# A fused two-layer perceiver: 16-head attention by query tiles, the 4-head attention's first pair entered early, bias rows on Pool, side steps in new places

## Chip, cores and metric

The kernel runs on one core of a Trainium2 chip. The metric is the device time of one execution in microseconds. Before the change the median of 3 runs is 592.93 (592.2 to 593.36).

## What is computed

The input `x` (2 batches of 256 rows, 256 wide, float32) goes through two layers; each step adds its result to `x`:

```python
x = x + xattn0(layernorm(x), ctx)        # scores over 4096 context rows per batch, values = ctx
x = x + linear_attention(layernorm(x))   # 64 heads of 4, cumulative sums
x = x + feed_forward(layernorm(x))       # 3 cycles of a gelu net that couples the two halves
x = x + xattn1(layernorm(x), ctx)
x = x + attn16(layernorm(x))             # 16 heads of rank 64: softmax(xQ (xK)^T / 16) x VO_h, summed
x = x + ffn(layernorm(x))
```

The last step is:

```python
def _mha(x, w, b, ow, ob):               # x is (L, N, D); attention runs over L
    L, N, _ = x.shape
    q, k, v = jnp.split(x @ w.T + b, 3, axis=-1)       # then 4 heads of 64
    attn = softmax(q k^T / sqrt(64))
    return (attn @ v) @ ow.T + ob
y1 = _ln(x + _mha(x, ...), ln1_g, ln1_b)
y2 = _ln(y1 + _moe(y1, ...), ln2_g, ln2_b)   # top-1 router, 8 experts of 64 places each
```

Here L is 2, the batches. So the 4-head attention of a row needs only the same row of the other batch: rows 0 to 127 of both batches are one pair of tiles (tiles 0 and 2, pair 0), rows 128 to 255 the other (tiles 1 and 3, pair 1). The 16-head attention needs all rows of its batch as keys, and each row only as a query.

## The kernel before, in words

All five engines have their own program; they meet at semaphores. The stages, with their times in the profiled execution:

- 0 to 30 us: start. Then **attention 0** to about 167 us: `attend(0, ...)` goes through 64 steps (`ORDER`), each a score or a value step of a query tile and a context chunk. Into it are put side steps: generators (`project`, `linear_attention`, `feed_forward`) of which `side_steps` advances one `yield` at the half steps that `SIDE_AT` lists for PE, ACT and DVE, each by itself. `PREP_AT` says at which steps ACT and DVE cut the next chunk of the context into two float16 halves; SP loads it, and turns it by DMA behind the cut.
- To about 218 us: **between**. Batch 0's side steps run out (the last feed-forward cycle, `project("y", 0)`), and batch 1's linear attention runs, in the order that the strings `BETWEEN` give for each engine ("y" is a step of batch 0's chain, "a" one of batch 1's).
- To about 347 us: **attention 1**, with batch 1's feed-forward, its projection and the entry of the 16-head attention as side steps. Then its projections, to about 369 us.
- To about 495 us: the **16-head loop** (`low_rank_attention`, PE from L641), 32 heads: 16 of batch 0, then 16 of batch 1, in 36 steps of a software pipeline. In step i PE does `scores5(i)` (two heads at a time, when i is even), `turn5(i-2)`, `mix5(i-3)` and `out5(i-4)`; DVE does the maximum, norm and low halves (`max5`, `norm5`, `lo5`, `oT_lo`), ACT the exponentials and high halves, Pool the low halves of the output weights. The outputs of all heads of a batch add up in one PSUM bank (6 or 7).
- Batch 0's rows leave this loop early. From step 20 on each engine advances its generator `enter_last` once at the end of each step (PE L759, DVE L1587): read of the bank and residual (`leave(0)`), layer norm, turn, and the projections of tiles 0 and 1 to q, k and v (PE L771 to L783, DVE L1562), through bank 6, in two pieces of 512 and 256 columns each.
- **The tail**, 495 to 535 us: `leave(1)` (L1551), layer norm "m" of batch 1 (L1270; Pool computes the reciprocal root, L1189), turn of tiles 2 and 3, their projections (PE L792 and L794). Then for each pair j: projection's bias add (L1623), products of queries and keys (pair 0 on DVE, pair 1 on Pool, L310), `scores6(j)` (L1628 to L1632), exponential on ACT, `values6(j)` (L1637 to L1647), turn (`turn_pair`, L756), output projection (L806), residual, output bias (L1664, L1665), statistics, norm (`norm_apply`, L1602 and L1606, with the root from Pool, L1245). DVE adds the bias of the second norm to X at L1658. After both pairs: turn, router's logits (L820), which DVE reads at L1677.
- To 592 us: **experts**: routing, and four pairs of experts, each with a matmul from 256 to 1024 (L864), a turn (L875), and one from 1024 to 256 (L889); combining (L898), second norm, store.

`keep_busy(n, bank)` (L410) issues n matmuls whose result nobody reads. What sets the order around the change are the programs of the engines themselves: everything behind a waiting instruction waits too. On SP's queue the weights of the last layer are loaded in program order behind the semaphores of L380 to L396. The memory of the expert weights 0 to 5 (`w2`, in `ctx_tr`) is that of the 16-head loop's tensors.

## Time and profile before

| | us |
|---|---|
| median of 3 runs (lowest to highest) | 592.93 (592.2 to 593.36) |
| the profiled execution | 593.91 |
| its span (first to last instruction) | 591.7 |
| PE busy | 522.6 (88%) |
| DVE busy | 366.1 (62%) |
| ACT busy | 282.7 (48%) |
| POOL busy | 70.1 (12%) |

PE is TensorE, DVE VectorE, ACT ScalarE, POOL GpSimd, SPq the queue in which SyncE issues DMAs. The time lies 2.2 us above the span: start and end of the execution. In the rows below "L732" is a line of the kernel; `out<-in` names what is written and read; a releaser behind `<-` in brackets is what ended the idle time before the instruction.

### The profile page before, as it was taken

To read this page: it belongs to the slowest core of one execution; us is meant where nothing else is said; L and a number is where in the kernel's file an instruction comes from. 1 tells how busy PE (TensorE), PEld (TensorE's weight loads), DVE (VectorE), ACT (ScalarE), POOL (GpSimd) and SP (SyncE) were. 2 spreads that over 40 slices of the span, in tenths; PEclk is the share of its full clock that TensorE was granted. 3 is DMA by queue.
4 is the path that set the end of the run, shared out by engine and by line. 5 is a ranking of instruction groups with operands and counts; after the bars stand their busy time and mean duration, and the time that the engine had idled before them with its cause. 6 is when DMAs were issued, how large, how long until landed. Compare 5 with 4: busy or idle time off the path is not lost.

```text
span 591.7 us, 9246 instructions
## 1 busy us (share of the span) xinstructions
PE 522.6 (88%) x3492; PEld 357.2 (60%) x3492; DVE 366.1 (62%) x855; ACT 282.7 (48%) x610; POOL 70.1 (12%) x59
## 2 busy tenths in 40 slices
PE   8599998999984779999989989699999998868993
PEld 6356664456642445657545777488888786654552
DVE  4665557864558555556465555688878773874335
ACT  3567852438812016674367736888554451012100
POOL 0114231200012100000002212333000000110001
PEclk9989999999996789999999999699999999989998
DMA  5658670000000010000320041221760136640001
GB/s 191 214 183 213 143 150 28 1 1 1 1 0 0 1 27 2 0 2 1 134 80 1 1 143 37 71 74 37 240 246 2 39 105 214 214 143 0 1 1 35
DMA packets 45196, 44.04 MB, mean 74 GB/s; under 512 B 18656, under 2 KB 41184, under 8 KB 45024
## 3 DMA queue, kind: packets, MB, share of 16 engines
q1 hardware_dynamic: 45152, 43.45, 23.8%
q8 instruction: 28, 0.46, 0.3%
q14 instruction: 16, 0.13, 0.1%
HBM read 38.73 MB, written 0.52 MB: 66 GB/s over the span
## 4 chain that ended last, share of the span: by engine, by line
PE 68%; DVE 16%; issue 8%; ACT 5%; DMA 2%; POOL 0%; SPq 0%; DVEq 0%; ACTq 0%; POOLq 0%
PE ps L590 9%; PE ps L720 7%; PE ps L619 7%; PE ps L732 7%; PE ps L604 4%; PE ps L621 4%; PE ps L679 4%; PE ps L706 3%; PE ps L864 2%; PE ps L889 2%; PE ps L694 2%; PE ps L483 2%; PE ps L437 2%; DVE work L1361 1%; DMA work<-in_ctx 1%
## 5 line engine op out<-in xcount | busy, mean ns | idle before, releaser
L590 PE MATMUL ps<-ctx_tr,qtl 128*128 128x512 f16 x384 | 91.7, 382 | 2.6 <-ACT arena L1039 2.1
L1427 DVE TENSOR_REDUCE mx<-arena 128x1 f32<-128x512 f32 x64 | 43.4, 683 | 34.2 <-ACT arena L1039 34.0
L590 PEld LDWEIGHTS ps<-ctx_tr,qtl 128*128 128x128 f16 x384 | 37.2, 99 | 41.5 <-issue 5.1
L1039 ACT ACTIVATE arena<-ps 128x512 f32<-128x512 f32 x64 | 38.0, 595 | 48.3 <-PE ps L590 48.2
L619 PE MATMUL ps<-ctx_nat,pth 128*128 128x512 f16 x172 | 58.2, 379 | 0.0
L1024 ACT ACTIVATE arena<-arena,small 128x512 f32<-128x512 f32 x64 | 45.8, 715 | 6.0 <-DVE small L1436 6.0
L732 PE MATMUL ps<-arena,ctx_tr 128*128 128x256 f16 x384 | 47.2, 273 | 0.1
L621 PE MATMUL ps<-ctx_nat,ptl 128*128 128x256 f16 x172 | 46.9, 273 | 0.0
L1189 POOL TENSOR_TENSOR rstd<-mv,col 128x2 f32<-128x2 f32 x12 | 9.2, 769 | 289.6 <-DVE mv L1280 289.6
L1441 DVE TENSOR_TENSOR ptl<-ps,pth 128x512 f16<-128x512 f32 x43 | 29.6, 689 | 22.3 <-ACT pth L1032 22.0
L604 PE MATMUL ps<-const,arena 128*128 128x128 f32 x256 | 39.0, 275 | 5.0 <-ACT arena L1024 2.8
L732 PEld LDWEIGHTS ps<-arena,ctx_tr 128*128 128x128 f16 x384 | 37.5, 98 | 4.7 <-DVE ctx_tr L1572 0.4
L604 PEld LDWEIGHTS ps<-const,arena 128*128 128x128 f32 x256 | 29.9, 140 | 16.7 <-ACT arena L1024 6.7
L1111 ACT ACTIVATE pth<-ps 128x512 f16<-128x512 f32 x32 | 19.0, 594 | 35.6 <-PE ps L706 35.6
L1104 ACT ACTIVATE ctx_tr<-ps,small 128x256 f32<-128x256 f32 x64 | 29.6, 470 | 5.9 <-DVE work L1531 5.9
L1032 ACT ACTIVATE pth<-ps 128x512 f16<-128x512 f32 x43 | 25.3, 589 | 13.3 <-PE ps L604 13.2
L1572 DVE TENSOR_TENSOR ctx_tr<-ps,ctx_tr 128x512 f16<-128x512 f32 x32 | 22.0, 689 | 13.0 <-ACT ctx_tr L1117 13.0
L1531 DVE TENSOR_SCALAR_CACHE_REDUCE work<-ps 128x256 f16<-128x256 f32 x64 | 24.4, 419 | 9.2 <-PE ps L694 9.1
L619 PE MATMUL ps<-ctx_nat,arena 128*128 128x512 f16 x84 | 28.6, 379 | 0.0
L619 PEld LDWEIGHTS ps<-ctx_nat,pth 128*128 128x128 f16 x172 | 16.8, 98 | 16.4 <-issue 0.4
L1441 DVE TENSOR_TENSOR arena<-ps,arena 128x512 f16<-128x512 f32 x21 | 14.5, 689 | 16.5 <-ACT arena L1032 16.3
L1544 DVE TENSOR_SCALAR ctx_tr<-ctx_tr,small 128x256 f32<-128x256 f32 x64 | 23.7, 412 | 1.1
(289 smaller groups left out, 1056.5 us busy)
## 6 DMA issues: line engine op xcount, KB each, us to landing
work<-in_ctx SPq DMA_DIRECT2D x16, 512.0 KB, 3.7
ctx_nat<-in_w_e SPq DMA_DIRECT2D x8, 1024.0 KB, 7.4
ctx_tr<-in_w_e SPq DMA_DIRECT2D x6, 1024.0 KB, 11.9
work<-in_w_vo SPq DMA_DIRECT2D x8, 512.0 KB, 3.8
ctx_nat<-in_w_l SPq DMA_DIRECT2D x4, 512.0 KB, 5.2
arena<-in_w_e SPq DMA_DIRECT2D x2, 1024.0 KB, 7.2
wts<-in_rows SPq DMA_DIRECT2D x1, 1024.0 KB, 7.2
arena<-in_w_a SPq DMA_DIRECT2D x1, 768.0 KB, 5.0
```

The costliest lines, as they stand in the source:

```text
L590: mm = pe.matmul(ps[:, n % 2, :], qtl[:, qh, d, u * P:(u + 1) * P], CT[:, t0:t0 + KT, kh, d, :], start=(i == 0 and d == 0), stop=(i == 2 a ...
L604: mm = pe.transpose(ps[:, 4 + j % 2, i * P:(i + 1) * P], S[:, (j) % SRING, i * P:(i + 1) * P], ident)
L619: pe.matmul(ps[:, acc, :], PH[j % PRING][:, i * P:(i + 1) * P], CN[:, t].rearrange("p h d -> p (h d)"), start=(c == 0 and i == 0), stop=Fa ...
L621: mm = pe.matmul(ps[:, acc, 0:D], PL[j % PRING][:, i * P:(i + 1) * P], CN[:, t, 0, :], start=False, stop=(c == NCH - 1 and i == KT - 1), s ...
L720: mm = pe.matmul(ps[:, 4 + i % 2, d * SEQ:(d + 1) * SEQ], xl5[b][:, xh, u, d * P:(d + 1) * P], pt[:, i % 2, pu], start=(n == 0), stop=(n = ...
L732: mm = pe.matmul(ps[:, 6 + b, t * D:(t + 1) * D], oT5[:, i % 2, oh, c, t * P:(t + 1) * P], vo[:, h, vh, c, :], start=(h == 0 and t == 0 an ...
L1024: act.activation(S[:, j % SRING, :], S[:, j % SRING, :], ACT.Exp, bias=ebias[:, u:u + 1], scale=SCALES[L], accum_out=ls[:, u, c:c + 1]).th ...
L1032: act.activation(PH[j % PRING], ps[:, 4 + j % 2, :], ACT.Copy).then_inc(s("pt_hi"), 1)
L1039: act.activation(S[:, n % SRING, :], ps[:, n % 2, :], ACT.Copy).then_inc(s("score_copied"), 1)
L1104: act.activation(P5[:, i % 2, t, :], ps[:, i % 2, t * SEQ:(t + 1) * SEQ], ACT.Exp, bias=nb5[:, i % 2, t:t + 1], scale=1.0 / 16, accum_out= ...
L1427: dve.tensor_reduce(mx[:, u, c:c + 1], S[:, n % SRING, :], AX.X, ALU.max).then_inc(s("score_max"), 1)
L1441: dve.tensor_tensor(PL[j % PRING], ps[:, 4 + j % 2, :], PH[j % PRING], ALU.subtract).then_inc(s("pt_lo"), 1)
```

## The change

It has five parts.

- **Query tiles.** For batch 1 the loop's step i no longer holds both query tiles of one head but one query tile of two heads: `in_step(i, p)`. The first 8 steps of batch 1 do tile 2 for all 16 heads, the last 8 do tile 3. The number of matmuls, turns and reads per step stays. PE waits for DVE's read of tile 2 (`x5`) before it writes tile 3's first output.
- **Pair 0 inside the loop.** `enter_last` goes on behind tiles 0 and 1: DVE reads tile 2 (`leave(1, slice(0, 1), H5 + 8)`), norms it, PE turns and projects it, Pool multiplies queries and keys of pair 0, DVE does `scores6(0)` and `values6(0)`, ACT the exponential, PE turn and output projection. The steps of each engine are placed by `LAST_AT` (half steps 0 to 71 of the loop) instead of one per step. The tail then holds tile 3's norm and projection, pair 0's residual and norm, and pair 1.
- **Pool** adds the output bias to `x0` and the second norm's bias to `X` (`biases`), six adds; DVE's adds at L1665 and L1658 go. Pool's product is now pair 0's, DVE computes pair 1's.
- **Side steps**: `SIDE_AT`, `BETWEEN`, `PREP_AT` have new numbers, and `Y0_AT` is 2: Pool's root for "y", 0 stands behind the second product of the linear attention of batch 1, not ahead of it.
- **Matmuls that keep PE busy**: 24, 56 and 36 become 18, 6, 30, 0 and 30. Tensors `P5`, `oT5`, `xl5[1]` and `prods[0]` lie elsewhere, and SP loads `w2[4]` and `w2[5]` behind the last head's output.

The diff, cut to what the text speaks of:

```diff
-Y0_AT = 1
+FILL = (18, 6, 30, 0, 30)
+LAST_AT = (
+    (49, 50, 51, 54, 55, 58, 59, 62, 70, 71,),
+    (65, 70,),
+    (43, 47, 48, 48, 50, 52, 54, 55, 55, 56, 57, 60, 62, 64, 67, 69,),
+)
+Y0_AT = 2
...
-PREP_AT = [0, 1, 2, 3, 4, 5, 6, 7, 9, 13, 15, 22, 24, 28, 30]
+PREP_AT = [0, 1, 2, 3, 4, 5, 6, 7, 9, 12, 13, 24, 27, 30, 31]
...
-            (1, 2, 4, 11, 16,),
-            (1, 2, 4, 11, 16,),
-            (1, 2, 5, 11, 16,),
+            (1, 3, 4, 11, 16,),
+            (0, 2, 4, 13, 16,),
+            (2, 2, 5, 12, 16,),
...
-    "yayaaayayaayyayyaaayyaaaa",
-    "aaayyayayaayayyaaayyaa",
-    "aaayyyaayaayayayayayayaaa",
+    "aayyayaaaayyyyayaaayyaaay",
+    "aaayaaaaaaaaayayayaaaayy",
+    "ayyaayaaaayyayyayayaayaaaa",
...
+        def in_step(i, p):
+
+            k = i - H5
+            return (i // 2, p) if k < 0 else (k % 8 // 2 * 2 + p, k // 8)
...
-            sp.wait_ge(s("l_vo"), H5 + H5 // 2)
+            sp.wait_ge(s("l_vo"), 2 * H5 - 4)
             load_w2(6)
             load_w2(7)
             sp.wait_ge(s("l_pv"), 2 * H5)
-            for e in range(6):
+            for e in range(4):
+                load_w2(e)
+            sp.wait_ge(s("l_vo"), 2 * H5)
+            for e in range(4, 6):
                 load_w2(e)
             sp.wait_ge(s("m_o"), 2)
...
+                    for p in range(2):
+                        j, t = in_step(i, p)
...
+                    pe.wait_ge(s("vo_lo"), min(i + 1, H5))
+                    if i == H5 + 8:
+                        pe.wait_ge(s("x5"), 2)
...
+                    for _ in range(LAST_AT[PE].count(2 * i)):
+                        next(early, None)
...
+            def leave_pair(j, b_turn, b_out):
+                pe.wait_ge(s("m_o"), j + 1)
+                turn_pair(o6, 0, b_turn, "m_oT_ps", j)
+                yield
+                pe.wait_ge(s("m_oT"), j + 1)
+                for b in range(B):
+                    t = 2 * b + j
+                    for c in range(DC):
+                        mm = pe.matmul(ps[:, b_out, b * D:(b + 1) * D], oT6[:, c, t * P:(t + 1) * P],
+                                       w6o[:, c, :], start=(c == 0), stop=(c == DC - 1))
+                mm.then_inc(s("m_out"), 1)
+                yield
+
             def enter_last():
...
+                for n in range(6):
                     t, cols = n // 2, ((0, 512), (512, 768))[n % 2]
-                    if n:
+                    if n == 4:
+                        turn_latents(1, (2,), 6)
+                        yield
+                    if n in (0, 4):
+                        pe.wait_ge(s("m_xT"), n // 4 + 1)
+                    else:
...
+                yield from leave_pair(0, 6, 6)
...
+                keep_busy(FILL[0], 2)
+                turn_latents(2, (3,), 3)
+                keep_busy(FILL[1], 2)
+                pe.wait_ge(s("m_xT"), 3)
+                for c in range(DC):
...
+                mm.then_inc(s("m_qkv_ps"), 1)
+                first_tiles()
+                for _ in leave_pair(1, 7, 3):
+                    pass
...
+            def first_tiles():
+                keep_busy(FILL[2], 2)
+                tiles_to_logits(0)
+                keep_busy(FILL[3], 2)
 
...
+            def biases(k, tiles):
+
+                w = [P, tiles.stop - tiles.start, D]
+                pool.wait_ge(s("w6_in"), 16 * 14)
+                pool.wait_ge(s("xn_turned"), NORM["m", k] + 1)
+                pool.tensor_tensor(x0[:, tiles, :], x0[:, tiles, :], b6o.unsqueeze(1).broadcast_to(w), ALU.add).then_inc(s("x_bo"), 1)
+                pool.tensor_tensor(X[:, tiles, :], X[:, tiles, :], ln2b.unsqueeze(1).broadcast_to(w), ALU.add).then_inc(s("x_beta"), 1)
+
+            layernorm("m", 0)
+            biases(0, slice(0, 2))
+            layernorm("m", 1)
+            biases(1, slice(2, 3))
+            pool.wait_ge(s("m_qkv0"), 6)
+            queries_times_keys(pool, 0).then_inc(s("m_prod"), 1)
+            layernorm("m", 2)
             for k, pair in enumerate((slice(0, NT, 2), slice(1, NT, 2), slice(0, 2), slice(2, 4))):
                 pool.wait_ge(s("m_var"), k + 1)
                 pool.tensor_tensor(rstd4[:, pair], mv4[:, pair, 1], nh, ALU.pow).then_inc(s("m_rstd"), 1)
+                if k == 0:
+                    biases(2, slice(3, 4))
 
 
...
+                def enter_last():
+                    dve.tensor_copy(ones16, ones[:, :])
+                    dve.tensor_copy(tris16, tris)
+                    dve.tensor_copy(id16, ident).then_inc(s("id16"), 1)
+                    leave(0, slice(0, 2), H5)
+                    yield
+                    yield from latents(0, (0, 1), 6)
+                    yield
+                    dve.wait_ge(s("w6_in"), 16 * 14)
+                    yield from project_early(range(4))
+                    leave(1, slice(0, 1), H5 + 8)
+                    yield from latents(1, (2,), 6)
+                    yield
+                    yield from project_early((4, 5))
+                    dve.wait_ge(s("m_prod"), 1)
+                    scores6(0)
+                    yield
+                    values6(0)
+                    yield
 
                 early = enter_last()
...
+                leave(1, slice(1, 2), 2 * H5)
+                entry = latents(2, (3,), 3)
+                next(entry)
+                for _ in early:
+                    pass
+                next(entry)
+                residual(0, 6)
+                for _ in entry:
+                    pass
...
+            def residual(j, n):
+                dve.wait_ge(s("m_out"), j + 1)
+                dve.wait_ge(s("x_bo"), B + 2 + j)
+                xs = x0[:, j:NT:2, :]
+                link(dve.tensor_tensor(xs, xs, bank(n, a=2), ALU.add))
+                norm_stats(x0, j, (j, 2 + j))
...
+                first_norm = norm_apply(x0, 0, (0, 2), ln1g, x0, lambda t: ln1b)
+                next(first_norm)
+                dve.wait_ge(s("m_qkv_ps"), 1)
+                link(dve.tensor_tensor(qkv[:, 3, :], ps[:, 0:2, :].rearrange("p b n -> p (b n)")[:, 0:768], b6i, ALU.add))
+                link(queries_times_keys(dve, 1))
                 scores6(1)
+                publish(next(first_norm), "m_y1")
                 values6(1)
+                residual(1, 3)
+                second_norm = norm_apply(x0, 1, (1, 3), ln1g, x0, lambda t: ln1b)
+                next(second_norm)
+                publish(next(second_norm), "m_y1")
```

## Rows read from the trace of the kernel before

**Rows 1.** Windows by stage: stretch, busy us (and instructions) of each engine, PEclk, DMA.

```profile
30.00:160.00 130.00, 123.24 (x707) 75.56 (x705) 80.50 (x152) 80.33 (x156) 23.68 (x13) 0.99 0.34 82
160.00:218.00 58.00, 38.41 (x133) 22.98 (x132) 34.21 (x67) 9.51 (x16) 6.63 (x5) 0.82 0.03 7
218.00:347.00 129.00, 123.61 (x706) 76.29 (x704) 72.57 (x150) 76.47 (x161) 11.28 (x11) 1.00 0.10 32
381.00:496.00 115.00, 114.90 (x1071) 97.36 (x1068) 89.85 (x275) 70.65 (x194) 12.25 (x11) 1.00 0.31 107
```

**Rows 2.** Chain of waits in the tail: start us, us, what.

```profile
493.78 1.50 PE ps L732 x12
495.30 0.70 DVE X L1551
...
497.75 0.70 POOL rstd L1189
...
505.36 0.97 DVE ctx_nat L1623
...
507.61 1.23 DVE work L1628
...
521.79 3.43 PE ps L806 x8
525.24 0.70 DVE ctx_tr L1664
...
527.84 0.88 DVE ctx_tr L1602 x2
```

**Rows 3.** Timeline of DVE in the tail: start us, us, instruction.

```profile
510.71 2.05 DVE L1639 TENSOR_TENSOR work<-work 128x16 f32<-128x16 f32 x1
...
517.72 0.16 DVE L1637 TENSOR_TENSOR work<-work 128x8 f32<-128x8 f32 x1
...
519.69 0.69 DVE L1647 TENSOR_TENSOR ctx_tr<-ctx_tr,arena 128x512 f32<-128x512 f32 x1
...
534.64 0.18 DVE L1677 COPY work<-ps 128x32 f32<-128x32 f32 x1
```

**Rows 4.** Chain of waits, projection of tile 0 in the loop.

```profile
455.64 1.72 PE ps L780 x4
```

**Rows 5.** Timeline of PE: pair 0 in the tail.

```profile
514.87 0.66 PE L756 MATMUL ps<-const,ctx_tr 128*128 128x128 f32 x4 [0.92 <-DVE ctx_tr L1647]
516.21 1.99 PE L806 MATMUL ps<-work,ctx_tr 128*128 128x256 f32 x8 [0.69 <-ACT ctx_tr L1138]
```

**Rows 6.** Windows ahead of and at the second output projection; PEclk follows POOL.

```profile
518.20:521.80 3.60, 0.67 (x6) 0.44 (x5) 3.46 (x6) 0.60 (x1) 0.00 (x0) 0.93 0.24 26
521.80:525.30 3.50, 3.50 (x11) 2.80 (x12) 1.26 (x7) 0.00 (x0) 0.69 (x1) 0.58 0.86 335
```

**Rows 7.** Timeline of POOL: the product of pair 1.

```profile
510.38 2.35 POOL L310 TENSOR_TENSOR arena<-ctx_nat 128x1024 f32<-128x1024 f32 x1 [11.94 <-DVE ctx_nat L1623]
```

**Rows 8.** Timeline of PE between the attentions, idle before in brackets.

```profile
187.65 1.11 PE L549 MATMUL ps<-const,arena 128*128 128x128 f32 x4 [8.04 <-DVE arena L1404]
...
195.68 0.66 PE L420 MATMUL ps<-const,wts 128*128 128x128 f32 x4 [2.65 <-DVE wts L1286]
198.09 3.78 PE L437 MATMUL ps<-arena,wts 128*128 128x256 f32 x8 [1.75 <-DVE arena L1293]
```

**Rows 9.** Timeline of DVE: the second tile's keys are ready.

```profile
188.67 0.42 DVE L1348 TENSOR_TENSOR work<-work,s 128x256 f32<-128x256 f32 x1
```

**Rows 10.** Timeline of POOL between the attentions.

```profile
191.83 2.01 POOL L1206 TENSOR_TENSOR work<-work 128x1024 f32<-128x1024 f32 x1
```

**Rows 11.** Timeline of PE in attention 0: wait for a score copy.

```profile
103.05 2.32 PE L590 MATMUL ps<-ctx_tr,qtl 128*128 128x512 f16 x10 [2.09 <-ACT arena L1039]
```

**Rows 12.** Timeline of SP's queue: issues of w2 0 to 5.

```profile
492.39 11.81 SPq L360 DMA_DIRECT2D ctx_tr<-in_w_e  x6
```

**Rows 13.** Chain of waits: first matmuls on w2.

```profile
552.58 3.45 PE ps L889 x31
```

More of the change, by code:

```diff
@@ new lines, in last_attention, with tiles_to_logits @@
+                for c in range(DC):
+                    mm = pe.matmul(ps[:, 1, 0:D], x0T[:, c, 3 * P:4 * P], w6i[:, c, 512:768], start=(c == 0), stop=(c == DC - 1))
+                mm.then_inc(s("m_qkv_ps"), 1)
+                first_tiles()
+                for _ in leave_pair(1, 7, 3):
+                    pass
+            def tiles_to_logits(j):
+                pe.wait_ge(s("m_y1"), j + 1)
+                turn_pair(x0, j, 4, "m_yT_ps", j)
+                pe.wait_ge(s("m_yT"), j + 1)
+                for t in (j, 2 + j):
@@ L791, in last_attention @@
                     for c in range(DC):
[L792 to L794 removed]
+                        mm = pe.matmul(ps[:, 6, t * E6:(t + 1) * E6], x0T[:, c, t * P:(t + 1) * P], wgt[:, c, :],
                                        start=(c == 0), stop=(c == DC - 1))
[L796 removed]
@@ L810, in experts @@
[L810 to L822 removed]
+                return mm
@@ L1132, in y_hi @@
                     act.activation(yy[:, g, 0], ys, ACT.Copy).then_inc(s("m_y_hi"), 1)
-                for j in range(2):
-                    act.wait_ge(s("m_sub"), j + 1)
-                    act.activation(sc[:, j], sc[:, j], ACT.Exp, scale=HD6 ** -0.5).then_inc(s("m_exp"), 1)
-                    act.wait_ge(s("m_oT_ps"), j + 1)
-                    act.activation(by_batch(oT6, j), ps[:, 6 + j, :].rearrange("p (c b n) -> p c b n", c=DC, b=B), ACT.Copy)\
-                        .then_inc(s("m_oT"), 1)
+                second = leave_pair(1, 7)
+                next(second)
                 for j in range(2):
@@ L1143, in last_part @@
                         .then_inc(s("m_yT"), 1)
-                for j in range(2):
-                    act.activation(y1[:, 0, j:NT:2, :], x0[:, j:NT:2, :], ACT.Copy).then_inc(s("m_y1_hi"), 1)
+                    if j == 0:
+                        next(second)
+                    else:
+                        for k in range(2):
+                            act.activation(y1[:, 0, k:NT:2, :], x0[:, k:NT:2, :], ACT.Copy).then_inc(s("m_y1_hi"), 1)
                 act.wait_ge(s("m_sub8"), 1)
@@ L1266, in _, with layernorm @@
             C = lambda name, n=P: col[0:n, COL[name]:COL[name] + 1]
-            def layernorm(what, b, to=None):
+            def layernorm(what, b, to=None, tiles=None):
                 k = NORM[what, b]
@@ L1273, in layernorm @@
                     dve.wait_ge(s("x_in%d" % b), 16)
-                for t in range(2):
-                    last = dve.bn_stats(bst[:, t, :], X[:, 2 * b + t, :])
+                tiles = (2 * b, 2 * b + 1) if tiles is None else tiles
+                for t, x in enumerate(tiles):
+                    last = dve.bn_stats(bst[:, t, :], X[:, x, :])
                 link(last)
-                for t in range(2):
+                for t in range(len(tiles)):
                     last = dve.bn_aggr(mv[:, t, :], bst[:, t, :])
@@ L1284, in layernorm @@
                     dve.wait_ge(s("xn_turned"), k)
-                for t in range(2):
-                    last = dve.tensor_scalar(to[:, t, :], X[:, 2 * b + t, :], mv[:, t, 0:1], rstd[:, t:t + 1],
+                for t, x in enumerate(tiles):
+                    last = dve.tensor_scalar(to[:, t, :], X[:, x, :], mv[:, t, 0:1], rstd[:, t:t + 1],
                                              ALU.subtract, ALU.mult)
@@ L1579, in low_rank_attention @@
                         norm5(i - 1)
+                    for _ in range(LAST_AT[DVE].count(2 * i)):
+                        next(early, None)
                     if 2 <= i <= 2 * H5 + 1:
```

229 lines of the change are left out of this document (85 added, 144 removed), and 12 rows, old and new, of the table SIDE_AT.

## The prediction, made before the changed kernel ran

> **What bounds the kernel now.** I read the time by stage first. In the three long stages TensorE is the bound: it is busy 123.2 of 130 us, 123.6 of 129 and 114.9 of 115 [rows 1]. The last of these is the loop of the 16-head attention; there DVE has 25 us free (89.9 of 115) and PE nothing. So side work put into that loop costs what it takes on PE, and what it takes on DVE is free while that slack lasts. Two stretches differ: the one between the two big attentions (PE 38.4 of 58 us) and the tail behind the loop, where the chain of waits runs from one engine to the next. The chain [rows 2] starts at T = 493.78 us with the last head's twelve matmuls and reaches the router's logits on DVE at 534.64 [rows 3]: 40.9 us for two pairs of query tiles, the second behind the first.
>
> **Part 1: the loop gets longer.** Tile 2 is projected in it (two matmul groups) and turned, and pair 0 is finished in it. The same projections of tiles 0 and 1 cost 1.72 us for 512 columns [rows 4], so about 0.86 for 256; turning one tile is half of 0.66 [rows 5]. Sum 2.9 us, all on PE, all on the path. On DVE the added steps are a few reads and norms of one tile, two bias adds, the scores (1.23 + 0.4 us) and the values of pair 0 (from 517.72 to the end of the 0.69 at 519.69, 2.66 us) [rows 2, 3]: together about 8 us (estimate), against 25 free. I followed the three step lists from step 25 on. PE meets no late operand until the end. There `values6(0)` stands ahead of the last head's `oT_lo`, and the turn of pair 0 ahead of the last head's matmuls: 1.0 us more before T. Bounds: 0.5 (the turn alone) and 2.7 (all of `values6`). The new wait of step 24's output on `x5` holds one PE queue, but DVE's read is asked for one step (about 3 us) earlier (114.9 us of PE for 36 steps): nothing. If that cover goes, it is a read of 0.5 us. Loop: +3.9 us. That scores and outputs go by query tiles leaves 12 matmuls for each two heads and 12 per head as they were: nothing.
>
> **Part 2: the tail from T.** Step by step, from rows:
> - last matmuls to DVE's first read: 1.5 (493.78 to 495.30).
> - read, statistics and epsilon up to Pool's power: 2.45 now for two tiles with three casts in between. One tile, without casts: 1.4, between 1.2 (half) and 2.45. Then Pool 0.7 and one tile's normalization 0.4. T + 4.0.
> - residual of pair 0 with its statistics: 525.24 to 527.84 is 2.6, less one add of 0.7 that moves to Pool: 1.9. Its operand, pair 0's projection, takes 2.0 on PE behind the last head and is ready. T + 5.9.
> - copy of tile 3 (0.4, half width) and its projection at the full clock, 2.6 + 0.2: T + 9.1. The first half of the norm of pair 0 and Pool's power and two adds lie beside it.
> - projection's add and the product of queries and keys: 505.36 to 507.61, 2.25; scores 1.65: T + 13.0.
> - second half of pair 0's norm 0.9, values of pair 1 2.66: T + 16.6.
> - turn and ACT's copy: 514.87 to 516.21, 1.34 [rows 5]: T + 17.9.
> - its eight matmuls: 1.99 at one clock [rows 5], 3.43 at the other [rows 2].
> - residual 1.9, norm in two halves 0.9 each, then 3.2 from the norm to the logits: 527.84 plus four halves is 531.4, and the logits are read at 534.64 [rows 2, 3].
> With 3.43 this is T + 28.3, so 12.6 less than 40.9; with 1.99 it is 14.0 less. I take 3.43: in the kernel before, PE was busy 0.67 of the 3.6 us ahead of such matmuls and the granted clock then fell to 0.58, the level of 1.2 GHz for most of it [rows 6]; in the changed order PE has about 2 us of work in the 5.6 us between its filler matmuls and these. **Loop and tail together: -8.7** (-10.1 with the full clock).
>
> **Part 3: Pool's adds.** Two adds of 128x512 leave DVE's chain for the output bias (0.7 each, in the sums above) and two for the second norm's bias, which lay where DVE waited for ACT. On Pool they are six: two of 512 and four of 256 columns. The nearest row is Pool's product of 1024 columns, 2.35 us [rows 7], so 1.2 and 0.6 each, 4.8 us in all, behind nothing that is due. Queued behind them are the power of tile 2's norm (six steps later) and the product of pair 0. What the row also shows: DVE's small multiply beside that product took 2.05 us instead of 0.2, and ended when Pool did [rows 3, 7]. In the loop Pool gets 3.6 us of adds and 2.35 of product, so DVE could be held 6 us; it has the slack, so I take nothing. The Trainium skill has a page that speaks against the change here: "SBUF — State Buffer", on who interferes with whom, says that a DVE instruction with two SBUF inputs or in a two-port mode is fully blocked while GpSimd reads SBUF. The row agrees with it; by that rule taken at its worst the sum is the rival B below.
>
> **Part 4: side steps placed anew.** In the stretch between the attentions PE waits 8.04 us for the last feed-forward cycle, then 2.65 for the next norm, then 1.75 [rows 8]. Now Pool multiplies the second tile's keys and values only after a power that waits for a later variance: DVE had its operand at 189.1, Pool began at 191.83 [rows 9, 10]. With Y0_AT = 2 the multiply goes first and the power starts about when it did. DVE normalizes ahead of the first running sum's reads, so PE turns that norm straight behind its sums at 193.0: the wait of 2.65 goes. The wait of 1.75 comes next and grows by 0.2, because the copy then stands behind DVE's reads. The 8.04 stays but for about 0.5 us, as the third feed-forward matmul is moved ahead of a projection. I take **-2.5**; bounds 0 and -3.2.
> Within the two big attentions PE idles 6.8 and 5.4 us in all [rows 1], of which a gain can be at most a part. Against it stands that a side step can block: at 103.05 PE had waited 2.09 us for a score copy, as ACT stood at a side step [rows 11]. No row prices the new places; I take nothing, and -4 to +4 for the range. The last two cuts of the context come two and three steps later in ACT's order, some 3 us; the scores that need them come seven steps on, so nothing.
> DMAs: experts' weights 4 and 5 now wait for the last head's output instead of its mixing, about 3 us later in SP's queue, and 6 and 7 for four heads more. The six loads were issued in 11.8 us from 492.39, and the first matmul on such weights ran at 552.58 [rows 12, 13]: even 10 us nearer they are covered. Nothing; if the cover went, the cost would be what the loads run past that matmul.
>
> **Sum.** -8.7 - 2.5 = -11.2 us on the profiled execution's 593.91 (span 591.7): 582.7. The median of the runs, 592.93, is 1.0 below it, so I forecast 581.7.
>
> **Rivals.**
> - A, the forecast: 577 to 585. Chance 0.62.
> - B, the port: Pool's reads hold DVE in the loop when a head is due, and the 6 us of part 3 all reach PE. 587.7. For: the 2.05 us row. Against: the loop's slack on DVE. Chance 0.11.
> - C, the new places inside the attentions cost what the stretch between gains, and some of the tail: 585 to 590, worked out as -11.2 + 2.5 + 2 = 586.2. Chance 0.12.
> - D, everything fits: full clock in the tail and 3 us out of the attentions' idle time, 577.3 and less. Chance 0.08.
> - E, slower: ACT stops at side steps ahead of score copies, 2.1 us on PE each time as at 103.05 [rows 11]. Six such stops more than before, one in every fifth or so of the 30-odd moved steps, cost 12.6 us: 594.3. From the sixth on it decides. For: three lists are moved and not all alike. Against: the kernel before has one such stop. Chance 0.04.
> - F, pair 0 isn't really inside the loop. Its turn and projection are PE's steps 70 and 71, at the last head. If `values6(0)` runs late, its 4.7 us of turn, copy and matmuls stand behind the loop: 586.4. Chance 0.03, and it counts with C. Of C's chance 0.03 lies beyond 591.7, where its price is double: 0.02 there is the same, 0.01 slower.
> The range takes A, B and most of C and D: 577.0 to 588.5. A measurement of this kernel can tell about 0.2%, 1.2 us, from no change: faster 0.93, same 0.02, slower 0.05.
>
> **What would show it.** Right: the loop without PE idle and 3 to 5 us longer; from the last head's matmuls to the logits 27 to 29 us; one projection of tile 3 in the tail; PE's turn of the second norm straight behind the running sum. Wrong: idle PE at the turns or mixes in the loop released by DVE (B); a span from 30 to 160 or 218 to 347 longer by over 2 us (C, E); in the tail a wait for pair 0's projection (F) or 1.2 GHz in tile 3's projection, 2.6 us more.

## The result, and the profile after

The changed kernel takes 578.27 us (577.6 to 582.76) against 592.57 before on the same chip: a ratio of 0.9756, 95% interval 0.9726 to 0.9785. The profiled execution took 577.76 us (span 575.9), half a microsecond under the median; 582.7 was the sum and 581.7 the forecast. Against the profiled execution of before, the span is 15.8 us shorter, 4.6 more than the 11.2 of the sum.

I cut both traces at the same instructions: the first turn of attention 0, a feed-forward matmul behind it, the last feed-forward cycle, the first score and the last turn's end of attention 1, the loop's start, T, and the logits on DVE. Windows by stage of the kernel before, columns as in [rows 1]:

```profile
49.57:136.89 87.32, 83.26 (x449) 48.43 (x449) 57.01 (x109) 48.29 (x99) 19.43 (x11) 1.00 0.35 79
136.89:187.65 50.76, 38.91 (x206) 24.75 (x205) 27.69 (x56) 27.55 (x54) 3.96 (x3) 0.96 0.00 0
187.65:217.65 30.00, 21.89 (x63) 13.92 (x63) 16.81 (x33) 1.19 (x2) 2.67 (x2) 0.73 0.05 14
...
373.88:493.78 119.90, 119.25 (x1085) 99.58 (x1085) 93.39 (x290) 76.15 (x208) 14.83 (x14) 0.97 0.30 101
493.78:534.64 40.86, 32.43 (x204) 24.60 (x205) 27.84 (x60) 3.86 (x8) 4.57 (x4) 0.92 0.62 206
```

And of the changed kernel:

```profile
47.47:133.57 86.10, 83.25 (x448) 48.37 (x448) 56.73 (x109) 48.46 (x101) 19.47 (x11) 1.00 0.38 80
133.57:183.06 49.49, 39.17 (x205) 24.89 (x205) 27.70 (x56) 24.70 (x50) 3.96 (x3) 0.94 0.00 0
183.06:209.96 26.90, 20.77 (x63) 13.38 (x64) 17.03 (x33) 1.08 (x2) 2.71 (x2) 0.75 0.05 15
...
366.12:489.81 123.69, 121.93 (x1098) 101.06 (x1098) 100.11 (x310) 76.49 (x210) 21.77 (x20) 0.98 0.30 99
489.81:518.72 28.91, 23.84 (x156) 18.79 (x157) 16.38 (x39) 3.61 (x7) 3.86 (x5) 0.93 0.86 285
```

The second number of a row is the length of its stretch. The loop grew by 3.79 us, and PE's busy time in it by 2.68. The granted clock of the two loops isn't the same (0.97 and 0.98); the section on the prediction sets this against loops of the same clock. The tail fell by 11.95. The three stretches ahead of 218 us fell by 1.22, 1.27 and 3.10. Ahead of the first turn 2.10 went; attention 1 and the experts' part moved by 0.1.

The chain of waits in the tail of the changed kernel can be laid beside part 2 of the prediction term by term (start us, us, what):

```profile
489.07 0.70 DVE ctx_tr L1652
...
489.81 1.50 PE ps L751 x12
...
491.34 0.44 DVE X L1611
...
492.73 0.71 POOL rstd L1235
...
493.79 0.69 DVE ctx_tr L1705
...
496.12 1.98 PE ps L831 x4
...
499.08 0.97 DVE ctx_nat L1735
...
506.63 0.67 PE ps L780 x4
...
507.98 3.60 PE ps L799 x8
...
511.66 0.70 DVE ctx_tr L1705
```

From T = 489.81 the first read comes at +1.5, pair 0's residual at +4.0, the add of the projection at +9.3, the turn of pair 1 at +16.8, the end of its projection at +21.8 and the logits at +28.9. The projection of pair 1 ran at 1.2 GHz, 3.60 us, as the sum had it.

### The profile page after: what moved, and what is told of

Read it like the earlier page. It is cut to its first block, busy times and chain, and to the rows that moved or that the text cites. A ratio compares the mean times of both kernels' runs of the same rounds, so it can differ in the third digit from the quotient of the medians.

```text
span 575.9 us, 9191 instructions
## 1 busy us (share of the span) xinstructions
PE 516.6 (90%) x3460; PEld 352.3 (61%) x3460; DVE 360.7 (63%) x855; ACT 279.7 (49%) x608; POOL 75.4 (13%) x66
## 4 chain that ended last, share of the span: by engine, by line
PE 67%; DVE 16%; issue 8%; ACT 5%; DMA 2%; POOL 1%; SPq 0%; DVEq 0%; ACTq 0%; POOLq 0%
PE ps L604 9%; PE ps L633 8%; PE ps L751 7%; PE ps L735 7%; PE ps L635 4%; PE ps L618 4%; PE ps L693 4%; PE ps L721 3%; PE ps L899 3%; PE ps L924 2%; PE ps L709 2%; DMA work<-in_ctx 2%; PE ps L819 1%; DVE mx L1487 1%; DVE work L1421 1%
## 5 line engine op out<-in xcount | busy, mean ns | idle before, releaser
L1501 DVE TENSOR_TENSOR ptl<-ps,pth 128x512 f16<-128x512 f32 x43 | 29.5, 688 | 22.7 <-ACT pth L1067 22.5
L1139 ACT ACTIVATE ctx_tr<-ps,small 128x256 f32<-128x256 f32 x64 | 29.6, 470 | 5.2 <-DVE work L1591 5.2
L633 PEld LDWEIGHTS ps<-ctx_nat,pth 128*128 128x128 f16 x172 | 16.8, 98 | 16.7 <-issue 1.0
L1501 DVE TENSOR_TENSOR arena<-ps,arena 128x512 f16<-128x512 f32 x21 | 14.5, 690 | 18.0 <-ACT arena L1067 17.9
L1282 POOL TENSOR_TENSOR arena<-work,arena 128x512 f16<-128x512 f32 x16 | 18.5, 1155 | 46.9 <-ACT arena L1119 46.9
```

The source lines that it names most:

```text
L633: pe.matmul(ps[:, acc, :], PH[j % PRING][:, i * P:(i + 1) * P], CN[:, t].rearrange("p h d -> p (h d)"), start=(c == 0 and i == 0), stop=Fa ...
L1139: act.activation(P5[:, i % 2, t, :], ps[:, i % 2, t * SEQ:(t + 1) * SEQ], ACT.Exp, bias=nb5[:, i % 2, t:t + 1], scale=1.0 / 16, accum_out= ...
L1501: dve.tensor_tensor(PL[j % PRING], ps[:, 4 + j % 2, :], PH[j % PRING], ALU.subtract).then_inc(s("pt_lo"), 1)
```

## The experiments

Ratios are to the kernel before, run beside each group; its own median lies between 592.0 and 593.8 us from group to group, so terms are read in the stretches of the traces. The changed kernel's 0.9756 is the mark, and where the interval of a ratio overlaps its interval (0.9726 to 0.9785), the ratio alone doesn't tell the two apart.

**1. The four lists of places back in the changed kernel.**

SIDE_AT and BETWEEN too are those of the kernel before, and:

```diff
-Y0_AT = 2
+Y0_AT = 1
...
-PREP_AT = [0, 1, 2, 3, 4, 5, 6, 7, 9, 12, 13, 24, 27, 30, 31]
+PREP_AT = [0, 1, 2, 3, 4, 5, 6, 7, 9, 13, 15, 22, 24, 28, 30]
```

> The changed kernel with the four old lists of places (before the loop it is then the kernel before, in the loop and the tail the changed one). Theory: the profiles differ by 7.7 us ahead of the loop (first turn 2.1 earlier, attention 0 another 1.9, between the attentions 3.7), and the new places make all of it: this run is 7.7 us slower than the changed kernel, about 585.5, and its gain over the kernel before, 8 us, is the tail and the loop alone. Rival 1: the 2.1 us ahead of the first turn are the landing times of the inputs and no work of the places: 5.6 us slower, 583.5. Rival 2 (my prediction's terms): only the stretch between gains, 2.5: 580.5.

0.9864 (0.9827 to 0.9901): 8.1 us less than before, 6.4 more than the changed kernel. The loop and the tail together take what they take in the changed kernel (152.6 us, against 160.8 before: 8.2 us), so this part stands by itself. The first turn started at 48.74.

**2. The same lists in the kernel before.**

> The kernel before with the four new lists of places. Theory: the same 7.7 us, 585 against 592.7, and the loop and the tail as they were (119.9 and 40.9 us). Rival 1 (landing times): 587. Rival 2: 590. If this and the run with the old places give different gains, the parts are not independent, and the profile has to show where one leans on the other.

0.9908 (0.9875 to 0.9941), 5.5 us less; loop and tail 160.7 us, as before. The two halves add up: 8.1 + 5.5 = 13.6, against 14.5 for the change (2.44% of 592.57). From the first turn to the first score of attention 1 it takes 162.6 us, the changed kernel 162.5, experiment 1 166.3 and the kernel before 168.1. So the places are worth 4 to 5.6 us there. That leaves the 2.1 ahead of the first turn. Experiment 4 shows where 4 and 5.6 part.

**3. The start and the two halves of attention 0.** The changed kernel with PREP_AT and the first lists of before, and with the second lists of before:

```diff
-            (1, 3, 4, 11, 16,),
-            (0, 2, 4, 13, 16,),
-            (2, 2, 5, 12, 16,),
+            (1, 2, 4, 11, 16,),
+            (1, 2, 4, 11, 16,),
+            (1, 2, 5, 11, 16,),
...
-            (66, 66, 69, 71, 72, 72, 74, 75, 77, 80, 83, 83, 87, 88, 90, 96, 97, 99, 99, 103, 104, 104, 105, 107, 110,
+            (63, 66, 69, 71, 71, 71, 72, 74, 75, 80, 82, 86, 87, 88, 88, 95, 96, 96, 97, 102, 104, 105, 105, 107, 108,
...
```

> The changed kernel with PREP_AT and the lists of the first half of the first attention (SIDE_AT[0][0]) of before. In all profiles with the new lists the first turn starts at 46.6 to 49.4 us (eight kernels, mean 47.6), with the old ones at 48.7 and 49.6; the first attention behind it, up to a feed-forward matmul at 133 us, takes 86.1 with the new and 87.3 with the old. Theory: the start is the landing of the inputs and not the lists, and the 1.2 us are these lists (the waits for cuts): first turn anywhere from 46.6 to 49.6, then 87.3, and about 1.2 us slower in all. Rival: the 1.2 us are the second half's lists: 86.1 here.

> The changed kernel with the lists of the second half of the first attention (SIDE_AT[0][1]) of before. Theory: the 1.3 us between the feed-forward matmul at 133 and the last wait of 8 us (49.5 us with the new places, 50.8 with the old) are these lists, and nothing else moves: 1.3 us slower. Rival: those come from the lists of the stretch between: 49.5 here, and no slower.

0.9782 (0.9743 to 0.9822) and 0.9806 (0.9774 to 0.9837). The rival of the first holds: with the first lists of before, the stretch up to the feed-forward matmul is still 86.1 us; with the second lists it is 87.3, and up to the last feed-forward cycle 137.3 us from the first turn, against 135.6 changed and 138.1 before. So the second lists made 1.7 of those 2.5 us. Where they did shows in PE's waits of more than 0.25 us between the first turn and the last cycle's: they add up to 6.52 us with the second lists of before and to 4.52 in the changed kernel. Timelines of PE with the second lists of before, then of the changed kernel (idle before in brackets; four of its waits each):

```profile
104.51 3.40 PE L573 MATMUL ps<-ctx_tr,qtl 128*128 128x512 f16 x15 [2.08 <-ACT arena L1043]
...
143.01 0.65 PE L517 MATMUL ps<-wts 128*64 128x256 f32 x2 [0.36 <-ACT wts L993]
...
163.53 0.65 PE L517 MATMUL ps<-wts 128*64 128x256 f32 x2 [0.96 <-ACT wts L993]
...
164.73 0.70 PE L526 MATMUL ps<-wts 64*128 64x256 f32 x2 [0.56 <-ACT wts L999]
```

```profile
98.19 1.46 PE L604 MATMUL ps<-ctx_tr,qtl 128*128 128x512 f16 x6 [0.88 <-ACT arena L1074]
100.69 3.40 PE L604 MATMUL ps<-ctx_tr,qtl 128*128 128x512 f16 x15 [1.05 <-ACT arena L1074]
...
136.50 1.13 PE L541 MATMUL ps<-wts 128*128 128x256 f32 x4 [0.59 <-ACT wts L1017]
...
156.38 1.13 PE L541 MATMUL ps<-wts 128*128 128x256 f32 x4 [0.28 <-ACT wts L1017]
```

The first wait is that of [rows 11], which I had used against the change. The new places hardly shorten it: 2.08 us in one piece became 0.88 and 1.05. The gain lies later, in the feed-forward's waits for ACT: 0.36, 0.96 and 0.56 became 0.59 and 0.28. Another 0.75 us of the 2.5 is still gained with the second lists of before. There PE waits 0.21 us for DVE ahead of one of the feed-forward's matmul groups, where the kernel before waits 0.79. The lists of the stretch between are the likely cause; no run has them alone.

The start is little or no part of the change. With one and the same set of first lists, profiled executions started their first turn anywhere from 46.6 to 51.0 us (eleven of them, half at 47.5 or earlier: the changed kernel 47.47, the kernel of experiment 6 with the same lists 49.40); with the old ones it was 48.74, 49.57 and 50.60. Three against eleven can't rule out a part of the lists in it. But the timed medians gave 14.3 us, and the trace has 13.7 behind its first turn, which leaves about half a microsecond for the start. What differs is, in part at least, how long ACT waits for the DMA of a context tile. Timelines of ACT, changed kernel and experiment 6:

```profile
25.37 1.06 ACT L1047 ACTIVATE ctx_nat<-work 128x1024 f16<-128x1024 f32 x1 [2.61 <-DMA work<-in_ctx]
```

```profile
25.86 1.06 ACT L1051 ACTIVATE ctx_nat<-work 128x1024 f16<-128x1024 f32 x1 [3.73 <-DMA work<-in_ctx]
```

**4. Y0_AT alone back at 1.**

> The changed kernel with only Y0_AT back at 1, so that Pool's power comes ahead of its second multiplication. Theory (the prediction's): the wait of 2.65 us for the second norm's turn went through this, and comes back, about 2 to 2.5 us: 580.5. Rival: the lists of the stretch between (DVE's norm ahead of its reads of the running sum) made it, and Pool's order is nearly free: within 0.5 us of the changed kernel.

0.9817 (0.9788 to 0.9845). Timelines of PE, and of Pool and DVE, between the attentions, this run, to be read against [rows 8]:

```profile
182.67 1.12 PE L563 MATMUL ps<-const,arena 128*128 128x128 f32 x4 [8.09 <-DVE arena L1464]
183.57 4.04 PE L497 MATMUL ps<-work,const 128*128 128x512 f32 x6
189.38 0.66 PE L434 MATMUL ps<-const,wts 128*128 128x128 f32 x4 [1.77 <-DVE wts L1346]
```

```profile
186.85 2.00 POOL L1252 TENSOR_TENSOR work<-work 128x1024 f32<-128x1024 f32 x1
186.92 2.41 DVE L1346 TENSOR_SCALAR wts<-X,mv,rstd 128x256 f32<-128x256 f32 x2 [0.82 <-POOL rstd L1235]
```

The turn of the norm comes 6.7 us behind the turn of the feed-forward cycle's result, in the changed kernel 5.2. So Y0_AT is worth 1.5 us beside the new lists, but not in the way predicted. The two normalizations of that norm, which DVE does right behind Pool's power, take 2.41 us here, and 0.74 in the changed kernel: the first began 0.07 us behind Pool's product of 1024 columns and ended 0.14 behind it. With Y0_AT = 2 the product is over before the power, and nothing holds them. Experiment 7 brings this hold about on purpose.

The strings of BETWEEN do their part too. With the old ones DVE normalizes behind its reads of the running sums, and the turn stands 2.65 us behind the six matmuls of those sums, however long they take: 4.47 us in the profile of before (turn at 8.0 us), 3.26 in experiment 1 (turn at 6.8), at other granted clocks. With the new ones DVE normalizes ahead of those reads, and the turn came at 5.16 or 5.17 us in all eleven kernels that have the new strings of BETWEEN and Y0_AT at 2, while their sums took 3.3 to 4.5 us. So the two together are worth 2.9 us against the profile of before and 1.7 against experiment 1. That is most of what parts 5.6 from 4 us in experiment 2.

**5. More fillers at one place.**

```diff
-FILL = (18, 6, 30, 0, 30)
+FILL = (18, 6, 44, 0, 30)
```

> The changed kernel with 44 instead of 30 filler matmuls ahead of the turn of pair 0's norm in the tail. In the changed kernel PE is idle there until 505.6 us and the eight matmuls of pair 1's projection then take 3.59 us at 1.2 GHz, against 1.99 at 2.4. Theory: with PE busy up to the turn the clock stays up and the projection takes 2.0: 1.5 us faster, 576.8. Rival 1: the idle stretch behind the turn (1.7 us of work in 2.4) lowers the clock all the same: 0. Rival 2: the fillers run beyond the moment at which the norm is ready and delay it: 0.5 us slower.

0.9782 (0.9762 to 0.9803), no gain. PE is now busy up to the turn of pair 0's norm at 504.62, but for 0.16 us, and the granted clock still falls behind it: the turn of pair 1 takes 1.11 us instead of 0.66. The idle pieces of PE between the fillers and that turn are 0.16, 0.69 and 0.30 us. From T to the logits it takes 29.56 us, what experiment 4 took too, whose tail is that of the changed kernel and whose clock was as low (0.88 over the stretch, against 0.93 in the changed kernel's 28.91). Timeline of PE:

```profile
507.32 1.11 PE L780 MATMUL ps<-const,ctx_tr 128*128 128x128 f32 x4 [0.30 <-DVE ctx_tr L1699]
509.12 3.78 PE L799 MATMUL ps<-work,ctx_tr 128*128 128x256 f32 x8 [0.69 <-ACT ctx_tr L1172]
```

**6. Fillers in every gap.**

```diff
+FILL = (18, 6, 44, 2, 30)
                 turn_pair(x0, j, 4, "m_yT_ps", j)
+                if j == 0:
+                    keep_busy(5, 2)
...
                 turn_pair(o6, 0, b_turn, "m_oT_ps", j)
+                if j:
+                    keep_busy(5, 2)
```

> The changed kernel with filler matmuls in each gap of PE from the projection of tile 3 to pair 1's output projection: 44 ahead of the turn of pair 0's norm, 5 behind it, 2 behind the first logits, 5 behind the turn of pair 1. 44 alone did not keep the clock: the eight matmuls took 3.78 us at a granted clock of 0.50, after 0.82 in the 2 us before. Theory: what lowered it are the gaps of 0.7 to 1.7 us behind that turn; with these filled the projection takes 2.0 us: 1.6 us less from the last head to the logits than 28.9. Rival: the fall doesn't hang on these gaps, or the fillers themselves stand in the way of the turns (0.1 to 0.3 us each): 0 or slower by up to 0.5.

0.9714 (0.9688 to 0.9739). This interval still overlaps the changed kernel's. But experiment 8, which measured the same as the changed kernel, ran on the same chip: its times are 578.1 to 580.5 us, those of this one 575.3 to 577.8, so this one is faster. From T to the logits it takes 27.3 us instead of 28.9, the 1.6 expected, at a granted clock of 1.00. Timeline of PE, and the windows at the projection (columns as in [rows 1]):

```profile
506.95 1.06 PE L849 MATMUL ps<-wts,ctx_tr 128*128 128x8 f32 x8
507.87 0.38 PE L424 MATMUL ps<-ones 128*128 128x256 f16 x2
508.31 0.66 PE L780 MATMUL ps<-const,ctx_tr 128*128 128x128 f32 x4
508.81 0.71 PE L424 MATMUL ps<-ones 128*128 128x256 f16 x5
509.65 1.99 PE L801 MATMUL ps<-work,ctx_tr 128*128 128x256 f32 x8
```

```profile
508.00:510.00 2.00, 1.79 (x14) 1.20 (x12) 0.26 (x1) 0.60 (x1) 0.00 (x0) 1.00 0.77 236
510.00:512.00 2.00, 2.00 (x13) 1.68 (x12) 0.26 (x1) 0.00 (x0) 0.00 (x0) 1.00 1.00 368
```

**7. The port: twelve more products on Pool in the loop.**

```diff
+            busy = prods[0].rearrange("p (a b) -> p a b", a=8)
+            one = ident.unsqueeze(1).broadcast_to([P, 8, P])
+            for k in range(12):
+                pool.tensor_tensor(busy, one, one, ALU.mult).then_inc(s("busy"), 1)
+                pool.wait_ge(s("busy"), k + 1)
```

> The changed kernel with twelve more products of 1024 columns on Pool in the loop, right behind its last subtraction of a head (406.8 us), which read and write SBUF: 12 x 2.35 = 28 us of Pool, over before the power at 444.5. All else is as it was. Theory (the prediction's): DVE's instructions in the loop mostly read PSUM and are not held, and where one is held DVE's slack of 25 us takes it: 0, and no PE idle between 405 and 436. Rival (the port, B of the prediction): DVE is held while Pool reads; with the lag that six microseconds were to give priced at one for one, 28 us of Pool cost up to 28, and a few us at least, and PE's idle time in that stretch shows DVE as releaser.

0.9937 (0.9905 to 0.9969): the loop takes 133.6 us instead of 123.7. My theory fell, the rival's mechanism is real. Timeline of DVE (out and in are named; `small` holds the softmax divisors):

```profile
410.87 3.92 DVE L1610 TENSOR_SCALAR ctx_tr<-ctx_tr,small 128x256 f32<-128x256 f32 x2
414.72 0.68 DVE L1602 TENSOR_TENSOR ptl<-ps,pth 128x512 f16<-128x512 f32 x1
```

The two normalizations, which read and write SBUF and take 0.62 us for both in quiet parts of the loop, take 3.92, two whole Pool products of 1.97 each. The next instruction, which takes an operand from PSUM, is as long as ever (0.68). So one pair per head is held, by up to the length of two Pool instructions, and PE waits for it, 2.52, 1.76 and 2.52 us ahead of three turns of the loop that DVE's normalization releases: in 405 to 430 us PE is busy 18.1 of 25, where it is busy all 25 in the changed kernel. The price depends less on Pool's total than on what it runs when a normalization is due.

In the changed kernel itself the new Pool work misses those moments. Timeline of DVE and POOL, changed kernel:

```profile
478.33 2.35 POOL L321 TENSOR_TENSOR ctx_nat<-ctx_nat 128x1024 f32<-128x1024 f32 x1 [8.71 <-DVE ctx_nat L1625]
479.65 0.69 DVE L1652 TENSOR_TENSOR ctx_tr<-ps,ctx_tr 128x512 f16<-128x512 f32 x1 [0.80 <-ACT ctx_tr L1152]
...
480.45 0.64 DVE L1604 TENSOR_SCALAR ctx_tr<-ctx_tr,small 128x256 f32<-128x256 f32 x2
```

The longest of the normalizations beside its adds and its product took 0.71; beside Pool's subtractions for the heads, in the first third of the loop of both kernels, it is up to 1.31. The Trainium skill's page "SBUF — State Buffer", on who interferes with whom, says that where such instructions of DVE and GpSimd meet, the one that issues first has the shared ports for its whole length and the other is fully blocked; my prediction had quoted it without the order. The trace agrees: here the Pool product was the first, and the pair took 3.92 us.

**8. The bias rows on DVE.**

```diff
+                    dve.tensor_tensor(x0[:, ts, :], x0[:, ts, :], b6o.unsqueeze(1).broadcast_to(to), ALU.add).then_inc(s("x_bo"), 1)
+                    dve.tensor_tensor(X[:, ts, :], X[:, ts, :], ln2b.unsqueeze(1).broadcast_to(to), ALU.add).then_inc(s("x_beta"), 1)
...
-                pool.tensor_tensor(x0[:, tiles, :], x0[:, tiles, :], b6o.unsqueeze(1).broadcast_to(w), ALU.add).then_inc(s("x_bo"), 1)
-                pool.tensor_tensor(X[:, tiles, :], X[:, tiles, :], ln2b.unsqueeze(1).broadcast_to(w), ALU.add).then_inc(s("x_beta"), 1)
```

> The changed kernel with the six adds of bias rows on DVE instead of Pool, right behind each copy of the turned latents. Theory: DVE's slack in the loop hides the four of the first two norms; the two of tile 3 stand in the tail ahead of the first residual's statistics or of the projection's add, 0.4 us each by the row of a 256-column add: 0.4 to 0.8 us slower in the tail, loop unchanged. Rival: the adds delay a due head's step in the loop as well, 1 to 3 us on PE.

0.976 (0.9736 to 0.9784): the same as the changed kernel. Loop 123.7, tail 28.8. Even the two adds of tile 3 cost nothing, since DVE waits for its projection anyway, 2.22 us in the changed kernel and 1.55 here. What the tail gained was that the adds are made earlier, not that Pool makes them.

**9. Pair 0's turn and projection behind the loop** (LAST_AT without PE's 70 and 71, ACT's 70, DVE's 69; ACT too finishes its generator behind the loop).

> The changed kernel in which the values of pair 0, their turn, copy and output projection are not placed in the loop but drained behind it (LAST_AT without DVE's 69, ACT's 70, PE's 70 and 71). It measures rival F and the term of 1.0 us that I gave the loop for them. Theory: the loop's last head starts 1.6 us earlier (0.66 turn, 1.0 values), but values, turn, copy and eight matmuls then stand ahead of the first residual, which comes 6 us later: 4 to 5 us slower in all. Rival: they find room in DVE's and PE's idle time of the tail: within 1.5 us of the changed kernel.

0.9791 (0.9747 to 0.9836), and 1.4 us more from T to the logits; the rival's bound holds. Of the 1.4, 1.0 is there when DVE adds the projection's bias (T + 10.3 instead of 9.3); the other 0.4 comes with the turn and projection of pair 1, which ran at a lower clock than in the changed kernel (0.88 us and 3.78 for 0.66 and 3.59). I had misread two things. DVE's 69 is an empty step: the values are placed at 67, so they stayed where they were. And T did not come earlier, since DVE's subtraction of the last head ends at T, turn or no turn: the turn of 0.66 lies beside it. In the changed kernel's chain above the subtraction is the 0.70 at 489.07 and T is 489.81; its timeline of PE has the turn between them:

```profile
489.09 0.66 PE L780 MATMUL ps<-const,ctx_tr 128*128 128x128 f32 x4
```

**10. The values of pair 0 really behind the last head.**

```diff
-    (49, 50, 51, 54, 55, 58, 59, 62, 70, 71,),
+    (49, 50, 51, 54, 55, 58, 59, 62, 71, 71,),
...
-    (43, 47, 48, 48, 50, 52, 54, 55, 55, 56, 57, 60, 62, 64, 67, 69,),
+    (43, 47, 48, 48, 50, 52, 54, 55, 55, 56, 57, 60, 62, 64, 69, 69,),
```

> The changed kernel with the values of pair 0 on DVE behind the last head's subtraction instead of ahead of it, and PE's turn of pair 0 behind the last head's matmuls. In the changed kernel ACT's half of the last head was there 0.7 us before DVE came to it, so the term of 1.0 us of my prediction should be 0.7. Theory: the last head starts 0.7 us earlier; in the tail tile 3's residual starts 1.2 us later behind the values (they fill 1.5 us of DVE's wait), pair 0's projection ends 0.8 us past its need: 1.3 us slower in all. Rival: tile 3's chain has room and it is the same or faster.

0.9828 (0.9792 to 0.9863). From the loop's start to that subtraction it takes 122.58 us. The changed kernel took 122.95, but at a higher granted clock; the second run of experiment 3, whose loop had the clock of this one (0.97), took 123.29. So the subtraction comes 0.7 us earlier, as expected; from it to the logits it takes 2.4 more. Timeline of DVE:

```profile
490.74 0.69 DVE L1652 TENSOR_TENSOR ctx_tr<-ps,ctx_tr 128x512 f16<-128x512 f32 x1 [1.93 <-ACT ctx_tr L1152]
...
494.03 0.43 DVE L1611 SCALAR_TENSOR_TENSOR X<-ps,X 128x256 f32<-128x256 f32 x1
...
497.43 0.69 DVE L1705 TENSOR_TENSOR ctx_tr<-ctx_tr,ps 128x512 f32<-128x512 f32 x1 [0.86 <-PE ps L799]
```

DVE waits 1.93 us for ACT, then does the values in a row while tile 3's read waits; and PE projects pair 0 just when tile 3 wants its turn. The direction was right, the size 0.4 us too small. Placing the values ahead of the last head is worth 1.7 us at the same clock.

**11. The best version: experiment 6 with another order in the tail.**

```diff
+FILL = (9, 6, 0, 28, 30)
...
+                residual_add(0, 6)
                 for _ in entry:
                     pass
+                norm_stats(x0, 0, (0, 2))
...
+                publish(next(first_norm), "m_y1")
                 dve.wait_ge(s("m_qkv_ps"), 1)
+                link(dve.tensor_tensor(qkv[:, 3, 0:512], ps[:, 0, :], b6i[:, 0:512], ALU.add))
                 link(queries_times_keys(dve, 1))
                 scores6(1)
+                dve.wait_ge(s("m_qkv_ps"), 2)
+                link(dve.tensor_tensor(qkv[:, 3, 512:768], ps[:, 1, 0:D], b6i[:, 512:768], ALU.add))
```

> The kernel with the gaps of PE filled (0.9714 of before), with the tail's order changed besides: 9 instead of 18 fillers ahead of tile 3's turn, its copy ahead of pair 0's statistics (the turn came 0.9 us late behind the fillers), queries and keys of tile 3 added before the values are projected (the add started 1.1 us behind the first matmul group's end), pair 0's norm finished in the wait for the projection instead of behind the scores (0.88 us on the chain, of which the values' add of 0.4 takes half). Theory: 0.95 + 1.1 + 0.4 - 0.35 = 2.1 us less from the last head to the logits, 27.3 to 25.2, and 574.3 us. Rival: pair 0's first residual or its norm is then what comes last, and under half of it is gained: over 26.3.

0.9691 (0.9665 to 0.9717), 574.03 us: the lowest of all, though its interval overlaps that of experiment 6. From T to the logits 26.5 us, 0.85 less than in experiment 6 where 2.1 were expected. Timeline of DVE and POOL:

```profile
495.33 0.72 POOL L1295 TENSOR_TENSOR ctx_tr<-ctx_tr,wts 128x256 f32<-128x256 f32 x1
495.47 1.73 DVE L1736 SCALAR_TENSOR_TENSOR ctx_tr<-ctx_tr,work,wts 128x256 f32<-128x256 f32 x2 [0.25 <-POOL work L1307]
496.01 0.90 POOL L1296 TENSOR_TENSOR X<-X,wts 128x256 f32<-128x256 f32 x1
497.23 0.69 DVE L1745 TENSOR_TENSOR ctx_nat<-ps,wts 128x512 f32<-128x512 f32 x1
```

Brought forward, the second half of pair 0's norm meets Pool's two adds of tile 3's bias rows and takes 1.73 us instead of 0.88; the add of queries and keys is behind it. That is 0.85 of the 1.25 us missing. Up to another 0.2 is the turn of pair 1, which came at 504.21 behind the 28 fillers, with the values ready at 504.00. The projection of pair 1 kept its 1.99 us, with no filler ahead of the turn of pair 0's norm. By experiment 8 these two adds cost nothing on DVE; a version with them there was not run.

## Why the prediction was right, and where its terms were off

- **Part 1, the loop: +3.9, measured +3.79, and 4.1 to 4.4 at one clock.** The loop of before had a granted clock of 0.97 and the changed one 0.98. Three executions of the changed loop had 0.97 too (the second of experiment 3, experiments 4 and 5) and took 124.0 to 124.3 us. This is the first of them, with its tail behind it:

```profile
372.03:496.07 124.04, 122.93 (x1099) 101.51 (x1099) 100.02 (x310) 76.60 (x210) 21.78 (x20) 0.97 0.30 98
496.07:525.61 29.54, 25.02 (x158) 19.51 (x159) 16.37 (x39) 3.60 (x7) 3.86 (x5) 0.88 0.83 279
```

  PE's busy time rises by 3.7 us in it. Of this, 0.66 is the turn of pair 0, which lies beside DVE's subtraction and costs nothing; the other 3.0 stand against the 2.9 of the sum. The 1.0 that I gave to the values' place is 0.7 by experiment 10. The remaining 0.4 I can't assign.
- **Part 2, the tail: 28.3 from T, measured 28.9.** The terms up to the projection's add came within 0.2 us; from there to the second residual 0.35 is added, half of it in the projection (3.60 for 3.43), and 0.15 behind it. The projection ran at 1.2 GHz as taken. The idle pieces of PE ahead of it, behind its fillers, are 1.69, 0.69, 0.30 and 0.69 us; experiment 5 shows that the clock falls without the first of them, and experiment 6 that it stays when all are filled. Tails of the same code whose clock stayed low for longer took 29.5 to 29.6 us. Loop and tail: -8.7 predicted, -8.2 in the traces and -8.1 in experiment 1.
- **Part 3, the Pool: nothing, measured nothing, but not for the reason given.** I took DVE's slack of 25 us as cover. Experiment 7 shows that slack to be no cover: a held normalization reaches PE in the same head. What excused the change is where the Pool work falls, which I hadn't worked out; that the term came out right was luck. Rival B's price of one for one was too high (9.9 us for 23.6 us of Pool) and its mechanism right; its chance of 0.11 was not too much.
- **Part 4, the places: -2.5 predicted; -4 to -5.6 in the runs.** This is the term that was off. Between the attentions 2.5 was about right: the wait of 2.65 us fell to 0.45, and the turn of the norm came 2.9 us earlier, with DVE's norm ahead of its reads as described. But the part of Y0_AT in it had another mechanism than mine: not when the product is ready, but that Pool's product must not run beside DVE's normalization (experiment 4). Within attention 0 I took nothing for the lists of its second half, since no row priced the new places. Experiment 3 shows 1.7 us from just those lists, mostly in waits of the feed-forward for ACT, of which I had shown no row; the one stop that I had shown, [rows 11], I had used for rival E alone, and it stayed about as long. The bounds of -4 to +4 held the 1.7.
- **The rest.** The trace's 15.8 us are 4.6 more than the sum. Of these 2.1 lie ahead of the first turn (46.6 to 51.0 with the same lists), 1.7 are those lists, about 1.3 is what the rest ahead of attention 1 gave beyond its 2.5, and loop and tail give back 0.5. The timed medians have 14.3 us, 3.1 more than the sum.
- **Rivals.** D came nearest in size. Its 3 us out of the attentions' idle time came about (PE's waits of over 0.25 us from the first turn to the last cycle's fell from 7.35 to 4.52 us), but the tail had the low clock. F's price of 4.7 was 1.0 to 1.4 in experiment 9. E did not happen: the one stop it was drawn from came as two that are no longer together.

## What to carry to other kernels

Slack of an engine is not cover for a hold: ask which single instruction is held at the moment it is due, and keep Pool's SBUF work away from it. The order of two instructions on Pool can matter for the same reason: of Pool's product and power here, the product had to be over before the power that lets DVE go on. When side work is placed anew, list all waits that the old placement shows, the short ones too, and price them as possible gains and not only as a risk. And where a short chain alternates between engines ahead of a costly matmul group, the fillers belong in the gaps right ahead of the group: 14 more at the front did nothing (experiment 5), and with none there the group still ran in 1.99 us (experiment 11).

## What the runs showed that I had not expected

- DVE and Pool hold each other by instruction, and it matters who is first. Beside a Pool product that was already running, DVE's normalization ran up to that product's end (3.92 us instead of 0.62 for a pair, beside two products). In the changed kernel the second of DVE's two scalings on SBUF was running when Pool's add began at 496.47: the pair kept its 0.87, and Pool's add took 0.97 where 0.72 is its length elsewhere. In experiment 9 the same add began at 495.69, ahead of the second scaling, and the pair took 1.34. Pool's power of two columns held nobody here: it ran from 495.82 to 496.51 in the changed kernel, and the scaling that began at 495.99 took its usual 0.48.
- Executions of one code differ by more than most terms of this sum. The first turn comes at 46.6 to 51.0 us. Attention 1 took 155.7 to 156.3 us in eight kernels with the new lists, at a granted clock of 0.99, and 158.1 or 158.2 in the four others, at 0.97 or 0.98. So a term of one or two microseconds has to be read from stretches, and against an execution whose clock in that stretch was the same.
